# Earlier requests for one pair's query weights, and two TensorE waits moved to the products that read the data, in a two-layer attention kernel

## What is computed

```python
x = x + _L0_xattn_ref(_layernorm(x), ctx, Wq, bq, Wk, bk)
x = x + _L0_ffn_ref(_layernorm(x), A, B, Wr)
x = x + _L1_xattn_ref(_layernorm(x), ctx, ctx, mask, wq, wk, wv, wo, 0)
x = x + _L1_ffn_ref(_layernorm(x), route_w, A, Bw)
# in _L1_xattn_ref: 32 query heads of 128
q = (query @ wq).reshape(bs, sq, HQ, DK).transpose(0, 2, 1, 3)
q = apply_rope(q, pos)
```

## Time and profile before

| what | value |
|---|---|
| median of 3 runs | 1742.03 us (1741.55 to 1742.15) |
| the profiled execution | 1740.39 us, its span 1738.5 us |
| PE busy in the span | 1707.7 us (98%) |
| DVE, POOL, ACT busy | 1124.9 (65%), 898.1 (52%), 770.0 us (44%) |
| DMA | 241.37 MB, mean 139 GB/s |
| granted TensorE clock, mean | 0.998 |

### The profile page before, as it was taken

One profiled execution on the slowest core, in us unless ns is written; L12 is line 12 of the kernel. 1 busy time (PEld: TensorE's weight loads), 2 busy tenths in 40 slices (PEclk: granted clock), 3 DMA queues, 4 the chain that ended last, 5 costly groups with the idle time before them and its releaser, 6 DMA issues.

```text
span 1738.5 us, 26113 instructions
## 1 busy us (share of the span) xinstructions
PE 1707.7 (98%) x8772; PEld 1556.1 (90%) x8772; DVE 1124.9 (65%) x2207; ACT 770.0 (44%) x1615; POOL 898.1 (52%) x696
## 2 busy tenths in 40 slices
PE   7999999999999999999999999999999999999998
PEld 6999999999888888888989998889999999999986
DVE  7631275556633333334978788998888888888845
ACT  5211211002423223223322224588888888888724
POOL 3324522114622121211587785588887877878734
PEclk9999999999999999999999999999999999999999
DMA  4122333234734333432254434677777777777643
GB/s 137 59 61 84 127 117 106 83 99 132 225 120 130 114 115 121 130 112 85 75 147 112 125 108 140 182 200 201 190 190 192 192 189 194 192 193 192 164 111 107
DMA packets 177198, 241.37 MB, mean 139 GB/s; under 512 B 47312, under 2 KB 145872, under 8 KB 176064
## 3 DMA queue, kind: packets, MB, share of 16 engines
q1 hardware_dynamic: 177088, 239.99, 49.0%
HBM read 142.68 MB, written 46.92 MB: 109 GB/s over the span
## 4 chain that ended last, share of the span: by engine, by line
PE 79%; DVE 4%; POOL 2%; issue 2%; DMA 2%; ACT 1%; SPq 0%; DVEq 0%; ACTq 0%; POOLq 0%
PE bank L200 75%; PE bank L106 1%; PE bank L2595 1%; PE bank L186 1%; PE bank L2608 1%; DMA aw_weights_then_ctx_rows<-in_wq 1%; POOL shared_operand_low L329 1%; POOL w_first_low L1610 1%; DMA aw_weights_then_ctx_rows<-in_wk 0%; DVE q_crossed L859 0%; DVE q_crossed L858 0%; POOL w_rest_low L794 0%; PE bank L1287 0%; POOL ctx_raw L1616 0%; DVE e_scores L1975 0%
## 5 line engine op out<-in xcount | busy, mean ns | idle before, releaser
L329 POOL TENSOR_TENSOR shared_operand_low<-ctx_raw,shared_operand_high 128x768 fp32r<-128x768 f32 x64 | 119.8, 1883 | 194.0 <-ACT shared_operand_high L325 193.9
L200 PE MATMUL bank<-shared_operand_high,w_first_high 128*128 128x448 f32 (+1 forms) x548 | 198.9, 363 | 1.8 <-DVEq L810 0.7
L200 PE MATMUL bank<-shared_operand_high,w_first_low 128*128 128x448 f32 (+1 forms) x548 | 198.2, 362 | 0.0
L200 PE MATMUL bank<-shared_operand_low,w_first_high 128*128 128x448 f32 (+1 forms) x548 | 198.0, 361 | 0.0
L1983 ACT ACTIVATE e_scores<-e_scores,e_least 128x375 f32<-128x375 f32 x256 | 153.3, 600 | 38.5 <-DVE e_least L1975 38.3
L325 ACT ACTIVATE shared_operand_high<-ctx_raw 128x768 fp32r<-128x768 f32 x64 | 52.8, 843 | 206.8 <-DMA ctx_raw<-in_ctx_t 188.2
L1975 DVE CUSTOM_DVE_ANT_0 e_scores<-bank,e_mask_then_layer_ffn 128x375 f32<-128x375 f32 x256 | 134.8, 529 | 0.0
L200 PE MATMUL bank<-shared_operand_high,w_rest_high 128*128 128x376 f32 x384 | 128.7, 335 | 0.4 <-POOL w_rest_low L794 0.4
L200 PE MATMUL bank<-shared_operand_high,w_rest_low 128*128 128x376 f32 x384 | 128.6, 335 | 0.0
L200 PE MATMUL bank<-shared_operand_low,w_rest_high 128*128 128x376 f32 x384 | 128.6, 335 | 0.0
L2018 DVE STREAM_TRANSPOSE q_rotated_then_x_rows<-e_scores 128x768 f32<-128x768 f32 x128 | 124.1, 970 | 0.3 <-DVE e_scores L1996 0.3
(11 more groups left out here) (324 smaller groups left out, 5121.8 us busy)
## 6 DMA issues: line engine op xcount, KB each, us to landing
ctx_raw<-in_ctx_t SPq DMA_DIRECT2D x64, 384.0 KB, 3.6
e_shuffled_then_xn_t<-q_rotated_then_x_rows SPq DMA_DIRECT2D x128, 192.0 KB, 3.7
e_shuffled<-q_rotated_then_x_rows SPq DMA_DIRECT2D x128, 192.0 KB, 3.7
e_raw_wo<-in_wo SPq DMA_DIRECT2D x64, 256.0 KB, 4.0
aw_weights_then_ctx_rows<-in_wq SPq DMA_DIRECT2D x30, 512.0 KB, 4.1
q_rotated<-q_rotated_then_x_rows SPq DMA_DIRECT2D x64, 224.0 KB, 2.3
e_raw_then_a<-q_rotated SPq DMA_DIRECT2D x64, 224.0 KB, 3.8
v_rows<-v_out SPq DMA_DIRECT2D x48, 256.0 KB, 2.5
```

The source lines that it names most:

```text
L200: mm = pe.matmul(out, stationary[a], moving[b], start=(first and i == 0), stop=(last and i == 2))
L329: pool.tensor_tensor(k.ctx_ring[1][slot][:, 2 * j:2 * j + 2, :], k.c_raw[:, j % 2], f32(k.ctx_ring[0][slot][:, 2 * j:2 * j + 2, :]), ALU.s ...
```

## The change

`load_w(1, 0)` now stands before the store of unit 2 and `load_w(1, 1)` before the store of unit 3, where before both stood behind the four stores and the waits. TensorE's wait for both low sums of rows, in front of pair 2, is gone; instead the fifth product of pair 2 waits for `x_low` CH + 3 and the seventh for CH + 4.

```diff
         load_w(0, 0)
         load_w(0, 1)
         for unit, (t, h) in enumerate(FIRST):
+            if unit >= 2:
+                load_w(1, unit - 2)
             store(unit, 0, t, h)
...
         for s in k.k_stored:
             sp.wait_ge(s, 16 + 16 * BATCH * GROUPS // 4)
-        for t in range(2):
-            load_w(1, t)
         for t in range(2):
...
             bank_read(i, n)
+            if i == seven.FIRST and n in seven.BY_VECTOR:
+                pe.wait_ge(x_low, CH + 3 + seven.BY_VECTOR.index(n))
             if i == seven.FIRST and n in ("sixth", "third"):
                 pe.wait_ge(rows_low, 3 + (n == "third"))
...
                 half_tile(4 + 2 * t + h, 1, t, h)
-        pe.wait_ge(x_low, CH + 4)
         for i in seven.pairs:
```

## The result

The changed kernel takes 1745.97 us (median of 18 runs, 1743.27 to 1748.35), the one before 1741.61 (median of 18). The ratio is 1.0023, with a 95% interval of 1.0016 to 1.0029: slower by 2.8 to 5.1 us. The forecast was 1744.3, 2.3 us more, in a range of 1741.3 to 1746.2. The time lies in that range, in its upper part; the shift that was forecast, 2.3 us, is smaller than the least of the interval, 2.8.

What follows compares the result with a forecast made beforehand. TensorE, working 98% of the span, bounds the kernel; its pauses and the lower clock offer some 5.4 us at most. 0 (SP) + 0 (waits) + 2.3 us (pair 3) gives 1744.3 us, range 1741.3 to 1746.2.

Steps and rivals of the forecast that it cites:

- L1706's last piece ends: VectorE's eight low pieces for the fifth and seventh sums end at 865.5 instead of 860.05, 5.5 us late.
- second product, and the pause before it: In pair 2, TensorE waits from 863.6 to 867.4, 3.8 us, for VectorE's late rotation of unit 5.
- mask leaves: On SP the mask load leaves at 874.0, after unit 7's rotation and ahead of pair 3's weight transfers.
- POOL can start pair 3: Pair 3's second weight transfer lands at 883.6; POOL starts at 883.7 instead of 881.37.
- pair 3's first matmul: TensorE starts pair 3 at 886.4 against 884.05, 2.3 us later, and 2.68 us after POOL.
- The turns at the port: Before pair 2, each VectorE low piece waits for one POOL instruction at the shared SBUF port: seven at 1.64 us.
- The place of the loss: All gain from the early requests ends in TensorE's wait before pair 3, which starts 2.3 us later.
- Low "third" and the second request: POOL's low part of the third weight half ends at 874.6; pair 3's second transfer leaves right after, at 875.0.
- the landing of the first transfer behind the mask: Pair 3's first weight transfer lands 7.5 us after its issue, through the mask, at 882.1; the second 1.5 later.
- The rival with the clock: Lower clock follows the pause before pair 3, not pair 2's: 1.6 us more, +3.9 us, 1745.9; chance 0.18.
- The free port: VectorE's pieces lose little beside POOL, no stall at pair 2's second product: -2.5 us, 1739.5; chance 0.09.
- half a collision: POOL falls behind by its own idle, VectorE's delay is 3 instead of 5.5 us: about 0, 1741.9; chance 0.09.

Runs made afterwards that it cites:

- pool_held: Changed kernel, but POOL starts pair 2's first sum only when VectorE has made both low sums: 1742.72 us, ratio 1.0004 to the kernel before.
- mask_behind: Changed kernel with the 1500 KB mask loaded behind pair 3's two weight transfers instead of ahead: 1741.11 us, ratio 1.0000 to the kernel before.
- before_mask_behind: Kernel before the change with the mask loaded behind pair 3's two weight transfers: 1741.02 us, ratio 0.9994.
- both single parts: Kernel before with only the early requests: 1746.38 us, ratio 1.0023; and with only the moved waits: 1740.52 us, ratio 0.9995.
- changed_look_2: Changed kernel run again unaltered for one more trace: 1744.63 us, one run.
- changed_look_3: Changed kernel run again unaltered for one more trace: 1743.34 us, one run.
- requests_only: Changed kernel with TensorE's old wait for both low sums in front of pair 2: 1746.38 us, ratio 1.0023 to the kernel before.
- changed_again: Changed kernel run again unaltered for a second trace and time: 1747.47 us (median of ten), ratio 1.0028 to the kernel before.
- waits_only: Kernel before with TensorE's two waits moved to the products, weight requests where they were: 1740.52 us, ratio 0.9995.
- no_pauses_2: As no_pauses, but VectorE makes the third sum's low pieces behind the rotation of pair 2's second product: 1739.15 us, ratio 0.9981 to the kernel before.
- no_pauses: Changed kernel combining pool_held and mask_behind, third sum's four low pieces moved from POOL to VectorE: 1739.01 us, ratio 0.9986 to the kernel before.

## Why the prediction was right

The time lies in the range, and the first trace follows the forecast step by step. It is the shortest of 18 executions, so this close agreement of the end is in part luck; the steps up to the mask are alike in all traces of the changed kernel. In t (the forecast's times less 848.3):

| step | forecast | measured |
|---|---|---|
| POOL starts pair 2 | 5.3 | 5.30 |
| L1706's last piece ends | 17.2 | 17.2 |
| second product, and the pause before it | 19.1, 3.8 us | 19.10, 3.71 us |
| mask leaves | 25.7 | 25.70 |
| POOL can start pair 3 | 35.4 | 35.51 |
| pair 3's first matmul | 38.1 | 38.14 |

**The turns at the port.** Seven pieces, each waiting for one POOL instruction of 1.64 us, was the step that carried the forecast, and it was right to the tenth: the eight pieces of the first trace start at 854.3, 855.8, 857.4, 859.0, 860.7, 862.3, 863.9 and 865.6, and POOL's instructions beside them at 853.82, 855.32, 856.96, 858.59, 860.22, 861.86, 863.68 and 865.13, one for one. `pool_held` shows that it is POOL's working that slows VectorE, not the change of order or of place.

**The place of the loss.** That the loss arises at pair 3 and not at the stall is shown by `mask_behind` beside `before_mask_behind`. That the moved waits are worth nothing is shown by both single parts.

**Low "third" and the second request.** The forecast had low "third" done at 874.6 (t = 26.3) and the second transfer leaving at 875.0 (t = 26.7). In the first trace it was done at 876.45 (t = 26.4), but the request left only at 877.88 (t = 27.9), because the issue of the first one took 1.44 us. (The 27.9 in the expectation of `mask_behind` takes the end of low "fourth", 877.87, for that of low "third".)

```profile
L1610 POOL TENSOR_TENSOR w_first_low<-aw_weights_then_ctx_rows,w_first_high x1: 1676/1676/1676, 874.8 to 874.8; 128x512 fp32r<-128x512 f32 x1
...
L1468 SPq DMA_DIRECT2D aw_weights_then_ctx_rows<-in_wq x1: 1438/1438/1438, 876.3 to 876.3; - x1
```

Where the first issue took 0.4 us (`changed_look_2`, `changed_look_3`, `requests_only`), the second request left at t = 26.8, as forecast. Why an issue takes longer in some executions stays open. It didn't matter here: the second transfer was ready 1.3 to 1.6 us behind the first in all five traces (ACT's and POOL's first instruction for pair 3, 883.98 and 885.53 in the first), whenever it had left. The 1.5 us of the forecast was right.

**What was mis-sized: the landing of the first transfer behind the mask.** The forecast took 7.5 us for it, from the one transfer of the kernel before that stood behind the mask, and came to 35.4 for POOL. In the four traces of the changed kernel it took 7.6, 10.0, 8.2 and 7.8 us, and 8.7 in `requests_only`, a mean of 8.5. So POOL's start of pair 3 was at 35.5, 37.7, 36.0, 35.6 and 36.3, though the mask left within 0.1 us of the same t: 0.1 to 2.3 us later than forecast, a mean of 0.8. It is the whole row that moves: the mask itself took 6.9 us to land in the first trace and 9.1 in `changed_again`. Pair 3's first matmul in the middle of the five traces is thus 3.1 us later than before, not 2.3.

**The rival with the clock** came true in part. It asked for no fall behind the first pause and one behind the second; in `changed_again` and `requests_only` both came. There, pair 3 pays 2.65 and 1.4 us more (to its seventh product 12.63 and 11.41 us instead of 9.98). Over five traces that is 0.8 us on average, which with the 3.1 gives 3.9, against 4.0 us by the ratio (2.8 to 5.1). The kernel before has only one trace in this sum; `waits_only`, which takes as long, has pair 3 at 35.1 instead of 35.8, so the agreement is no better than 0.7 us. The forecast had taken the two falls to exclude each other, which was an error of reasoning: a fall behind the first pause shortens the second, but it doesn't keep the clock from falling again. The traces of the changed kernel are mostly of its shorter executions (three of four under the median), so how often the second fall comes isn't settled by five traces.

**The free port and half a collision** didn't occur in any trace of the changed kernel: the eight pieces took 13.0 us in each of the four.

## What to carry to other kernels

Starting an engine sooner was worth nothing by itself here: list what it will run beside. Here POOL's idle 2.6 us were the time in which VectorE did five of its eight pieces at a third of the cost. When an engine becomes late, the price need not be the first wait that shows up; here it was the longest row of transfers behind it. Follow it through every queue, and look for a large transfer that nobody needs soon standing in front of a small one that is needed: moving it is a single line.

## What the runs showed of the hardware

- A two-operand VectorE piece of 448 columns between SBUF tiles took 0.61 us alone and 1.54 to 1.72 us beside a busy POOL, in every trace (one piece of 1.08 us in `no_pauses_2` is the exception). The rotation's products, with one operand in PSUM (L857 to L859), stayed at 0.61 to 0.63 us beside the same POOL.
- The granted clock's fall does not go by the length of the pause alone. In pair 2 it fell behind pauses of 1.83 us (`no_pauses`, t = 29.1, 1.5 us after TensorE had gone on), 2.74 (`waits_only`), 2.82, 2.83, 3.33, and behind or within all of 3.39 and more; it did not fall behind 2.75 (`before_mask_behind`). Before pair 3 it fell behind 2.30 (`requests_only`) and within 4.84 (`changed_again`), and not behind 1.69, 2.58 and 3.08. Mostly it stayed down for 3.4 us, at a cost of 1.4 to 1.7 us where TensorE works throughout; in three places (pair 3 of `changed_again`, pair 2 of `requests_only` and of `changed_look_3`) it stayed down for 6.8 us, and cost 2.65 in the first. In this kernel a pause of 2 to 3 us therefore has to be priced with a chance, not with a rule.
- Behind the same 1500 KB in the queue, the landing of a 512 KB transfer moved by 2.2 us between executions of one kernel (POOL at 35.5 to 37.7). Why it moves stays open; of the changed kernel with only the mask moved there is one trace, at 32.3.
